# Attention with relative positions: one value bank for two groups of heads, near scores in token order, one subtraction

## The reference

```
x: [16, 512, 128], 16 heads of 8 features
xn = layernorm(x);  Q, K, V = xn @ W + b
idx = clip(k - q, -2, 2) + 2
scores = (Q.K + Q.rel_k_table[idx]) / sqrt(8), causal mask
attn = softmax(scores)
out = attn @ V + attn @ rel_v_table[idx]
x = x + layernorm(out @ W_o + b_o)
```

## Time and profile before

| | |
|---|---|
| runs | 1035.07, 1040.36, 1035.12 us; median 1035.12 |
| span of the profiled execution | 1036.5 us, mean granted TensorE clock 0.960 |
| its own time | not marked among the three runs; the span is 1.4 us above the median |
| busy | PE 86%, DVE 80%, ACT 65%, POOL 70% |
| attention stage | up to about 740 us, steps of 41.5 us |

### The profile page before, as it was taken

How to read it: one execution, slowest core, us unless ns; L and a number is a source line. 1 busy time by engine, 2 the same in 40 slices (tenths; PEclk the granted TensorE clock), 3 DMA queues, 4 the chain that set the end, 5 groups by cost and what they waited for, 6 DMA issues and landing times. The chain is left out here.

```text
span 1036.5 us, 23477 instructions
## 1 busy us (share of the span) xinstructions
PE 896.3 (86%) x7655; PEld 513.6 (50%) x7655; DVE 833.7 (80%) x1948; ACT 676.3 (65%) x1305; POOL 727.1 (70%) x940
## 2 busy tenths in 40 slices
PE   2778889889889898898898988986679999999995
PEld 0324444444444444444444444432457777777773
DVE  5578888888988888889888888877568788878884
ACT  2038677777676777776777777765447767676773
POOL 4135686876867868768678687576357989898886
PEclk9769999999999999999999999988889999999999
DMA  2610110110101101011011011101425455555441
GB/s 48 170 44 34 35 44 31 47 42 32 49 31 42 45 32 47 32 43 49 32 42 44 33 47 40 35 18 50 148 59 169 144 165 150 169 151 166 162 140 31
DMA packets 64004, 74.93 MB, mean 72 GB/s; under 512 B 10032, under 2 KB 39600, under 8 KB 63904
## 3 DMA queue, kind: packets, MB, share of 16 engines
q1 hardware_dynamic: 61536, 73.17, 22.4%
q10 hardware_dynamic: 2368, 0.48, 0.3%
HBM read 43.75 MB, written 8.65 MB: 51 GB/s over the span
## 5 line engine op out<-in xcount | busy, mean ns | idle before, releaser
L1128 DVE TENSOR_REDUCE mx<-ps_s 128x1 f32<-128x512 f32 (+2 forms) x640 | 408.6, 681 | 84.3 <-PE ps_s L1540 83.7
L799 ACT ACTIVATE prob<-ps_e 128x512 f32<-128x512 f32 x640 | 349.6, 606 | 103.3 <-PE ps_e L1497 103.2
L641 POOL TENSOR_SCALAR_AFFINE_SELECT prob<-prob 128x516 f32<-128x516 f32 (+1 forms) x320 | 174.9, 571 | 141.8 <-ACT prob L799 141.8
L1519 PE MATMUL ps_s<-ks,qs 63*128 63x512 f16 (+3 forms) x1024 | 224.5, 312 | 47.4 <-DVE mx L1128 31.5
L1497 PE MATMUL ps_e<-qs,ks 64*128 64x512 f16 (+3 forms) x1024 | 212.1, 307 | 3.7 <-ACT prob L799 1.7
L721 POOL TENSOR_TENSOR hidden_low<-hidden,hidden_high 128x512 fp32r<-128x512 f32 x144 | 191.1, 1356 | 12.1 <-ACT hidden_high L989 10.9
L1557 PE MATMUL ps_av<-prob,vp 128*32 128x512 f32 (+3 forms) x2048 | 182.4, 452 | 4.3 <-POOL prob L641 4.2
L1519 PEld LDWEIGHTS ps_s<-ks,qs 63*128 63x128 f16 x1024 | 67.6, 95 | 184.0 <-DVE mx L1128 80.5
L989 ACT CAST hidden_high<-hidden 128x512 fp32r<-128x512 f32 x160 | 98.0, 612 | 30.5 <-DVE hidden L1441 27.3
L1540 PE MATMUL ps_s<-masked_at,below_r 64*128 64x128 bf16 (+3 forms) x640 | 103.1, 211 | 0.0
L1540 PE MATMUL ps_s<-masked_at,below 64*128 64x128 bf16 (+3 forms) x640 | 91.3, 213 | 0.0
(11 more groups left out here) (177 smaller groups left out, 1737.7 us busy)
## 6 DMA issues: line engine op xcount, KB each, us to landing
gate_rows<-gates_dram SPq DMA_DIRECT2D x128, 256.0 KB, 3.6
qs<-qh SPq DMA_DIRECT2D x128, 32.0 KB
qs<-ql SPq DMA_DIRECT2D x128, 32.0 KB
xnT_dram<-oT SPq DMA_DIRECT2D x16, 256.0 KB, 2.0
xeT<-xnT_dram SPq DMA_DIRECT2D x16, 256.0 KB, 2.7
out<-result SPq DMA_DIRECT2D x16, 256.0 KB, 2.3
v_near<-v_back SPq DMA_DIRECT2D x16, 254.0 KB
ks<-kh SPq DMA_DIRECT2D x124, 32.0 KB
```

The source lines that it names most:

```text
L641: pool.affine_select(out=v, in_=v, compare_op=ALU.is_ge, fill=0.0, base=-2, pattern=cols, channel_multiplier=-1).then_inc(S["p_masked"], 1)
L799: act.activation(prob[g % 2][:, u, b, :], ps_e[bank][:, :], ACT.Exp, scale=SCALE).then_inc(S["e_done"], 1)
L1128: dve.tensor_reduce(out, src, AX.X, ALU.max).then_inc(s_free[bank], 1)
L1519: pe.matmul(scores[:, at:at + P * (qt + 1)], qs[par][rows, 2 * g + off, P * qt:P * qt + P], ks[par][rows, 2 * g + off, 0:P * (qt + 1)], st ...
```

## The change

Two groups of four heads write one bank: `vp` keeps 32 columns per head, but in groups with an odd number the values and the ones stand 16 columns further right, so that the products of the second group are accumulated onto the first's and land in other rows. There are two copies, transposes and hand-overs per sequence instead of four (uses av0, av1). The near scores are summed with e0 and e1 as the weights and `head_sum` (already scaled) as the moving matrix, so that the result has tokens as rows; the ACT copy and the transposes go, and DVE reads it in step with maximum 5. The two differences are one subtraction with m16 broadcast.

```diff
-AT = {"e_sums": 1, "av2": 2, "m1": 4, "v0": 5, "av3": 6, "xT": 6, "s_tok": 7, "oT": 7, "q": 9,
-      "k": 10, "oproj": 11, "av0": 14, "m0": 15, "av1": 17, "xn2": 18, "logits": 19}
-STAGE = {"av2": "C", "e_sums": "A", "m1": "B", "s_tok": "A", "av3": "C", "v0": "A", "oT": "C", "xT": "F",
-         "oproj": "C", "q": "F", "k": "F", "av0": "B", "m0": "A", "av1": "B", "xn2": "C", "logits": "C"}
+AT = {"e_sums": 1, "m1": 4, "v0": 5, "av1": 6, "xT": 6, "oT": 7, "q": 9,
+      "k": 10, "oproj": 11, "m0": 15, "av0": 17, "xn2": 18, "logits": 19}
+STAGE = {"e_sums": "A", "m1": "B", "av1": "C", "v0": "A", "oT": "C", "xT": "F",
+         "oproj": "C", "q": "F", "k": "F", "m0": "A", "av0": "B", "xn2": "C", "logits": "C"}
...
-        vp = [sb(f"vp{i}", [P, NT, H, 32]) for i in range(2)]
+        vp = [sb(f"vp{i}", [P, NT * NGRP, 4, 2 * WIDE]) for i in range(2)]
...
-        den = sb("den", [P, NT, 8])
-        rden = sb("rden", [P, NT, 8])
-        num = sb("num", [P, NT, 8, D])
+        den = sb("den", [P, 2, NT, 4])
+        rden = sb("rden", [P, 2, NT, 4])
+        num = sb("num", [P, 2, NT, 4, D])
...
-                act.copy(vp[st.a % 2][:, :, :, 0:D].rearrange("p t h d -> p (t h) d"),
-                         ps_s[bank][:, :].rearrange("p (c d) -> p c d", d=D)).then_inc(S["v_ready"], 1)
+                    act.wait_ge(S["v_rows"], 3 * st.a + 3)
+                of = ps_s[bank][:, :].rearrange("p (c j d) -> p c j d", j=4, d=D)
+                for q in range(2):
+                    last = act.copy(vp[st.a % 2][:, q::2, :, WIDE * q:WIDE * q + D], of[:, q::2])
+                last.then_inc(S["v_ready"], 1)
...
-            def s_rows_out(st):
-
-
-                act.wait_ge(S["misc_full"], st.misc("e_sums") + 1)
-                act.activation(s_rows[:, :], ps_misc[0:64, :], ACT.Copy, scale=1.0 / M_UNIT).then_inc(S["misc_free"], 1)
-
-            def av_out(st, s, g):
-
-                act.wait_ge(S["av_full"], st.at(NGRP * s + g + 1, NGRP))
-                act.copy(av_s[g % 2][:, :], ps_av[:, :]).then_inc(S["av_copied"], 1)
+            def av_out(st, s, part):
+
+                act.wait_ge(S["av_full"], st.at(NGRP * s + 2 * part + 2, NGRP))
+                act.copy(av_s[part][:, :], ps_av[:, :]).then_inc(S["av_copied"], 1)
 
             def xn2T_out(st):
 
...
-                                        AX.X, ALU.add))
+                own.mark(dve.tensor_reduce(head_sum[:, :], head_sel[:, :, :, :].rearrange("p d pr b -> p (pr b) d"),
+                                           AX.X, ALU.add))
+                own.settle()
+                ready(dve.tensor_scalar(head_sum[:, :], head_sum[:, :], 1.0 / M_UNIT, None, ALU.mult))
                 for i in range(2):
                     ready(dve.tensor_tensor(dv[:, i, :].rearrange("p (h d) -> p h d", d=D),
                                             rv[:, i + 1, :].unsqueeze(1).to_broadcast([P, H, D]),
...
 
-                dve.wait_ge(S["misc_full"], st.misc("s_tok") + 1)
-                src = ps_misc[:, 0:NT * 64].rearrange("p (t n r) -> p n t r", t=NT, n=2)[:, :, :, 0:H]
-                own.mark(dve.tensor_copy(s_tok[:, 0], src[:, 0]))
+                dve.wait_ge(S["misc_full"], st.misc("e_sums") + 1)
+                src = ps_misc[:, 0:2 * NT * H].rearrange("p (n t h) -> p n t h", n=2, t=NT)
+                own.mark(dve.tensor_copy(s_tok[:, :, :, :], src))
                 own.settle()
-                own.mark(dve.tensor_tensor(s_best[:, :, :], s_tok[:, 0], src[:, 1], ALU.max))
-                dve.tensor_copy(s_tok[:, 1], src[:, 1]).then_inc(S["misc_free"], 1)
-
-                dve.wait_ge(S["misc_free"], st.misc("s_tok") + 1)
-                own.settle()
+                dve.tensor_tensor(s_best[:, :, :], s_tok[:, 0], src[:, 1], ALU.max).then_inc(S["misc_free"], 1)
+
+                dve.wait_ge(S["misc_free"], st.misc("e_sums") + 1)
 
             def max_half(st, s, half):
 
@@ -1153,40 +1144,31 @@
                 dve.scalar_tensor_tensor(m16[:, :, hs], mx[:, QT0:, hs], 1.0 / M_UNIT, s_best[:, :, hs],
                                          ALU.mult, ALU.max).then_inc(S["m16_ready"], 1)
                 dve.wait_ge(S["m16_ready"], st.at(2 * s + half + 1, 2))
-                for k in range(2):
-                    last = dve.scalar_tensor_tensor(d01[:, k, :, hs], m16[:, :, hs], -1.0, s_tok[:, k, :, hs],
-                                                    ALU.mult, ALU.add)
-                    if k == 0:
-                        own.mark(last)
-                last.then_inc(S["d_ready"], 1)
-
-            def av_tok_out(st, s, g):
-
-
-                dve.wait_ge(S["misc_full"], st.misc(f"av{g}") + 1)
-                if g == 0:
-                    dve.wait_ge(S["near_ready"], st.at(4 * s + 2, 4))
-                if g == 2:
-                    dve.wait_ge(S["near_ready"], st.at(4 * s + 4, 4))
-
-                if g % 2 == 0:
-                    need(dve, S["o_ready"], st.at(2 * s + g // 2, 2))
-                v = ps_misc[:, :].rearrange("p (t j c) -> p t j c", t=NT, j=4)
-                par, hs = s % 2, slice(4 * (g % 2), 4 * (g % 2) + 4)
-                own.mark(dve.tensor_tensor(den[:, :, hs], v[:, :, :, D], p_near[par][:, :, 4 * g:4 * g + 4], ALU.add))
-                cols = slice(4 * g * D, 4 * g * D + 4 * D)
-                dve.tensor_tensor(num[:, :, hs, :], v[:, :, :, 0:D], near[par][:, :, cols].rearrange(
-                    "p t (j d) -> p t j d", d=D), ALU.add).then_inc(S["misc_free"], 1)
-                if g % 2 == 0:
-                    return
+                dve.tensor_tensor(d01[:, :, :, hs], s_tok[:, :, :, hs],
+                                  m16[:, :, hs].unsqueeze(1).to_broadcast([P, 2, NT, 8]),
+                                  ALU.subtract).then_inc(S["d_ready"], 1)
+
+            def av_tok_out(st, s, part):
+
+                dve.wait_ge(S["misc_full"], st.misc(f"av{part}") + 1)
+                dve.wait_ge(S["near_ready"], st.at(4 * s + 2 * part + 2, 4))
+
+                need(dve, S["o_ready"], st.at(2 * s + part, 2))
+                par = s % 2
+                v = ps_misc[:, :].rearrange("p (t j q w) -> p q t j w", t=NT, j=4, q=2)
+                both = slice(8 * part, 8 * part + 8)
+                cols = slice(8 * part * D, 8 * part * D + 8 * D)
+                own.mark(dve.tensor_tensor(den[:, :, :, :], v[:, :, :, :, D], p_near[par][:, :, both].rearrange(
+                    "p t (q j) -> p q t j", q=2), ALU.add))
+                dve.tensor_tensor(num[:, :, :, :, :], v[:, :, :, :, 0:D], near[par][:, :, cols].rearrange(
+                    "p t (q j d) -> p q t j d", q=2, d=D), ALU.add).then_inc(S["misc_free"], 1)
                 own.settle()
-                own.mark(dve.reciprocal(rden[:, :, :], den[:, :, :]))
+                own.mark(dve.reciprocal(rden[:, :, :, :], den[:, :, :, :]))
                 own.settle()
 
-                dve.wait_ge(S["misc_free"], st.misc(f"av{g}") + 1)
-                both = slice(4 * (g - 1) * D, 4 * (g + 1) * D)
-                dve.tensor_tensor(o_tok[:, :, both].rearrange("p t (j d) -> p t j d", d=D), num[:, :, :, :],
-                                  rden[:, :, :].unsqueeze(3).to_broadcast([P, NT, 8, D]),
+                dve.wait_ge(S["misc_free"], st.misc(f"av{part}") + 1)
+                dve.tensor_tensor(o_tok[:, :, cols].rearrange("p t (q j d) -> p q t j d", q=2, d=D), num[:, :, :, :, :],
+                                  rden[:, :, :, :].unsqueeze(4).to_broadcast([P, 2, NT, 4, D]),
                                   ALU.mult).then_inc(S["o_ready"], 1)
 
             def y_out(st):
...
                 maxima(2, 3)
-                if st.C:
-                    av_tok_out(st, st.c, 2)
                 if st.t0 == NSEQ + 1:
 
                     dve.wait_ge(S["misc_free"], Step(NSEQ).misc("logits") + 1)
                     gates_scores(0, EARLY)
-                maxima(3, 7)
+                maxima(3, 5)
+                if st.A:
+                    s_tok_out(st)
+                maxima(5, 7)
...
                 if st.C:
-                    av_tok_out(st, st.c, 3)
+                    av_tok_out(st, st.c, 1)
...
-                maxima(13, 18)
-                if st.A:
-                    s_tok_out(st)
-                maxima(18, 22)
+                maxima(13, 22)
...
-                maxima(25, 28)
-                if st.B:
-                    av_tok_out(st, st.b, 0)
-                maxima(28, 30)
+                maxima(25, 30)
...
                 if st.B:
-                    av_tok_out(st, st.b, 1)
+                    av_tok_out(st, st.b, 0)
...
-                if kt == 0:
-
-                    need(pe, S["av_copied"], st.at(NGRP * s + g, NGRP))
+                if kt == 0 and g % 2 == 0:
+
+                    need(pe, S["av_copied"], st.at(NPART * s + g // 2, NPART))
...
-                    last = pe.matmul(ps_av[32 * j:32 * j + 32, P * kt:SEQ], vp[par][:, kt, 4 * g + j, :],
```

(29 more changed lines are left out.)

36 lines of the change are left out of this document (10 added, 26 removed).

## The result

The changed kernel takes 1047.45 us (median of 4 runs, 1043.0 to 1051.34), the kernel before 1036.91 us beside it: ratio 1.010, 95% interval 1.007 to 1.0129, so 1.0% slower. The forecast was 1024.8 us, faster. What follows reads one profiled execution of each kernel. That of the changed kernel is its fastest run, 1043.0 us with a span of 1041.3 us, so its books explain 4.8 of the 10.5 us between the medians; its other three runs aren't profiled.

The account below looks back on a forecast made before the run. No engine is full: PE and DVE are coupled, with two waits per step for POOL chains. Full steps at -0.49 us give -6.9, then +1.0, -3.9, -0.5: -10.3 us, 1024.8 us; forecast's own range 1020 to 1030, overall 1014 to 1033.

Parts of the forecast that it names:

- Slower: the clock (12%): Rival, 12%: thin e_sums behind the logits bring low clock; decides from 3 of 14 steps, at half of them 1049 us.
- three signs of being wrong: m1's transposes wait for s_tok; low clock in most steps; PE idle under 3.5 us with a step below 40.5.
- e_sums: Round 1: sixteen passes take 2.0 us where the old products took 0.98, +1.02 us per step.
- PE-bound: Round 1, e_sums: the stretch is limited by PE, so its +1.02 us counts in full.
- av2's transposes and the 0.23 us wait: Round 2: the transposes go, -0.59 us per step, and PE's wait for a maximum goes, -0.23 us.
- xn: Round 6, POOL chain: PE and stats1 both come 0.20 us later, so the wait stays and +0.20 passes through.
- s_tok's transposes: Round 7, PE-bound: they go, -0.39 us per step, with nothing late against it.
- Rounds 10 to 18: DVE, then POOL: POOL is first at the subtraction; DVE comes forward only until x1's statistics, -0.30 us per step.
- The tail: Step 17: router work starts earlier and av2's transposes go, -3.9 us; step 18: av2's transposes go, -0.5 us.
- The ramp: Two steps at the start with e_sums but no av2: 2 x (1.02 - 0.39) - 0.30 = +1.0 us.
- Both bottlenecks relax (14%): Rival, 14%: PE's waits behind maxima shrink by a third or passes cost half; step 1.1 to 1.3 us shorter, 1015 us.
- The single subtraction doesn't save what it seems to: First half of heads: behind POOL's subtraction it saves nothing; half of the four differences' 2 us per step, already in the forecast.

Follow-up runs that it names:

- round 8: The changed kernel with the sixteen thin e_sums passes moved from round 1 to round 8, s_tok on DVE before maximum 18 again: 1043.96 us, ratio 1.0054.

## Why the prediction was wrong

**The step that failed** is the choice between cases: the forecast left out the clock, and "Slower: the clock (12%)" is what happened. Its condition, three disturbed steps of fourteen, was met three times over (9 of 13). Its total, "7 x 3.5 = 24 us, 1049 us", lies close to the 25.3 us and 1047.45, and that is partly luck: it was nine steps at 2.8 us and not seven at 3.5, on a full-clock time that was forecast too high, and the execution with the 25.3 us took 1043.0. What the runs show in the place of "no clock": with the near sums as before the same kernel takes 1020.66 us, 26.8 less, at full clock. The argument against it was "the logits do the same today and the mean over ten steps is 0.99". That compared the new passes with passes elsewhere. It didn't ask what the edit took away beside them: two broad products of 0.98 us, in the stretch from round 18 to round 3 that holds the logits and the transposes, and where the earlier trace rows already had 0.54. Nor was that the only low stretch of the ten steps: there is another, from 232.6 to 236.0, in the same place right behind the logits. Two falls in one place were read as one exception.

Two of the prediction's three signs of being wrong came, too: low clock in most steps, and a step of 40.18 us in which PE idles 3.45 us.

**The sum at full clock** was too small, -0.49 us a step against 41.41 to 40.17 = -1.24. By its own terms:
- e_sums: forecast 2.0 us, measured 451.56 - 449.67 = 1.89. Right.
- "PE-bound" in round 1 was wrong. In the kernel before, round 1 took from 442.82 to 443.86, 1.04 us; after, from 451.56 to 452.22, 0.66. The timeline of the weight loads (PEld) of the kernel before shows why, where PE's rows show no wait:

```profile
443.42 0.09 PEld L1519 LDWEIGHTS ps_s<-ks,qs 63*128 63x128 f16 x1 [0.33 <-DVE mx L1128]
```

  So 0.38 us of e_sums' price were free, behind DVE; round 8 shows what it costs without that cover.
- av2's transposes and the 0.23 us wait went, as forecast; together with the last tenths of rounds 2 and 3, m1's transposes come 455.81 - 449.67 = 6.14 us after e_sums, where it was 448.43 - 441.84 = 6.59: -0.45 instead of +0.20.
- xn: the wait stays (0.90, now 0.89), and the difference passes through, as forecast.
- s_tok's transposes: -0.39, as forecast.
- Rounds 10 to 18: forecast -0.30, measured -0.40 (the step's -1.24 less -0.84 at the o_tok transposes). POOL is first, the remaining difference takes 1.00 us, DVE takes up x1's statistics 0.09 us behind POOL. All as forecast. This is where the Trainium skill's page "SBUF — State Buffer" (Who interferes with whom) was weighed, and the runs have both outcomes of its rule, that of two such instructions the one that starts second is held up: 1.00 us behind POOL in the change, 0.23 us when 0.01 us ahead of it with the subtraction alone (POOL's own then takes 1.12 us, beside 1.04 in the change).

**The ends.** The tail was forecast at -4.4 us (-3.9 and -0.5) and came to -4.6; the router work starts at the beginning, and PE's wait before the o_tok transposes of step 17 is 1.14 us instead of the 2.92 of the earlier trace rows. DVE's timeline, and PE's:

```profile
701.23 0.37 DVE L1147 TENSOR_TENSOR d<-s_tok,m 128x64 f32<-128x64 f32 x1
701.52 0.85 DVE L1233 TENSOR_SCALAR logit<-logit 128x448 f32<-128x448 f32 x1
```

```profile
711.46 0.63 PE L1542 MATMUL ps_e<-ident,o_tok 128*128 128x128 f32 x4 [1.14 <-DVE o_tok L1170]
```

The ramp was forecast at +1.0 and cost +4.5, of which the first e_sums, 2.8 us earlier, gives over half back. Here the term was priced at the wrong clock: in both kernels e_sums runs at half clock in these steps, 3.59 us in the change against 1.92 before, so two of them cost +3.3 us and not +2.0.

"Both bottlenecks relax (14%)" had the step right (1.1 to 1.3 us shorter) and the time wrong; its reason was right in part, PE's waits behind maxima going from 1.9 to 1.5 us in a step, a quarter less and not a third. "The single subtraction doesn't save what it seems to" held for the time (ratio 0.9973) for another reason than given: there DVE came first and the step was 0.71 us shorter, and the clock took it back.

**What stays open.** What the chip weighs when it lowers the clock isn't settled by these runs. A fall follows thin passes (the change) or a long wait (subtraction alone), and not every time. Which of the things that the near sums in the old form bring back (broad products, copy, transposes, the later s_tok) keeps the clock isn't isolated; a kernel with the thin passes and one pair of broad ones that nobody reads, and nothing else restored, would tell. The length of the step may have a part, too: it differs from kernel to kernel, and no run changes it alone. Nor is it settled why the value bank alone has half clock in each step from 311 us on, right behind the logits, for some 0.2 us each, and the same kernel with the single subtraction has it once.

## What to carry to other kernels

Count an edit's columns as well as its time: an operand swap that turned two broad products into sixteen thin passes shortened the step at full clock by 0.39 us, and 25 us went to the clock that it left. Low stretches in the clock of the kernel before, even one or two in ten steps, mark a place to be careful with: price an edit there at both clock levels. And whether a stretch is bound by PE is read from the weight loads' waits as well as from PE's own: one missed wait, 0.38 us by the length of the round, was half of the error of 0.75 us at full clock.

## What the runs showed of the hardware

- A thin fp32 pass with 128x128 weights costs the same for 8, 16 or 64 columns: 0.99 us for eight passes of 8, 1.89 us for sixteen of 16, 1.93 us for sixteen of 64, so 0.12 us each.
- The same sixteen thin passes go with different clocks in different surroundings: granted clock 0.95 with them in place of the broad products, 0.97 with 64 columns moving in place of 16, 0.99 with thin and broad ones, 1.00 with them in round 8 ahead of two projections.
- Thin passes aren't needed for it: with the subtraction alone, 1.2 us behind PE's wait of 1.37 us for a maximum, the clock was 0.50 (seen in the trace, not isolated, and the same wait stands in steps without a fall).
- Half clock isn't always a loss. With the value bank alone it comes in each step from 311 us on and costs some 0.2 us (a wait of 0.43 us for DVE that an undisturbed step has soon behind it is gone); in the change it costs 1.5 us where it begins behind e_sums (41.63 against 40.17), and 5.7 where it begins at the logits and takes e_sums in (42.60 + 43.46 against twice 40.17, since it lies across two of these distances).
